# Another periodic order for the steps of a convolution, attention and expert-routing kernel

## The reference

```
x = conv(x)        # channel norm, 1x1 conv, grouped 3x3 conv, softmax state over the image, h, y, 1x1 conv, + x
t = tokens(x)
u = ln(t); q, k, v = lrelu(u Wq + bq), lrelu(u Wk + bk), lrelu(u Wv + bv)
o = softmax(mask(q k^T / 8)) v + u
t = t + gamma * normalised(o) + beta
u = ln(t); expert = argmax(softmax(u gate_w + gate_b))     # 8 experts, capacity 5120 tokens
t = t + prob * (relu(u w1[expert] + b1) w2[expert] + b2)   # kept tokens only
```

## Time and profile before

| | |
|---|---|
| median of 3 runs | 2253.11 us (2244.7 to 2254.15) |
| the profiled execution: its own time, its span | 2252.71 us, 2251.0 us |
| granted TensorE clock, mean | 0.965 |
| busy share of the span: PE, DVE, ACT, POOL | 90%, 84%, 53%, 45% |
| `token_program` | 0 to about 1700 us of the span |
| `finish_program` | about 1700 to 2251 us |
| one period, mean of ten (748.35 to 1226.70 us) | 47.84 us |

### The profile page before, as it was taken

The page is one execution under the profiler, slowest core; times in us unless marked ns, Lnnn a source line. Parts: engine busy times, 40 slices in busy tenths (PEclk is TensorE's granted clock), DMA queues, the critical chain, the costliest instruction groups (busy, mean ns, idle before and its releaser), DMA issues. The chain is left out here.

```text
span 2251.0 us, 42376 instructions
## 1 busy us (share of the span) xinstructions
PE 2021.3 (90%) x13855; PEld 1643.0 (73%) x13855; DVE 1900.7 (84%) x6075; ACT 1196.8 (53%) x2216; POOL 1015.1 (45%) x1276
## 2 busy tenths in 40 slices
PE   1679999999999999999999999999837999999996
PEld 1357777777777777777777777777736999988895
DVE  3268889899998999899999999988865998998895
ACT  0135554555554554554554555554425777777773
POOL 3011443444443444443444434444363665555553
PEclk9679999999999999999999999999967999999998
DMA  4911211121211122111222211221116777877774
GB/s 173 365 48 29 67 48 48 49 71 54 57 57 48 51 74 58 50 56 48 60 65 58 58 48 48 62 67 37 37 35 182 205 222 256 263 248 257 256 246 175
DMA packets 163515, 244.00 MB, mean 108 GB/s; under 512 B 31039, under 2 KB 110478, under 8 KB 163296
## 3 DMA queue, kind: packets, MB, share of 16 engines
q1 hardware_dynamic: 146016, 209.46, 30.7%
q0 software_dynamic: 17280, 31.84, 4.3%
HBM read 115.95 MB, written 95.56 MB: 94 GB/s over the span
## 5 line engine op out<-in xcount | busy, mean ns | idle before, releaser
L1205 PE MATMUL pvp<-va,pT 128*128 128x129 f32 x4096 | 494.6, 276 | 0.6 <-ACT pT L741 0.4
L1205 PEld LDWEIGHTS pvp<-va,pT 128*128 128x128 f32 x4096 | 486.3, 193 | 10.3 <-issue 1.9
L741 ACT ACTIVATE pT<-stp 128x512 f32<-128x512 f32 x512 | 285.3, 595 | 251.4 <-PE stp L1179 245.6
L1376 POOL DMA_INDIRECT token_rows<-res x284 | 305.6, 1076 | 231.0 <-DVE res L1509 161.4
L855 DVE TENSOR_REDUCE mxs<-mxp 128x1 f32<-128x512 f32 x512 | 337.4, 683 | 17.4 <-PE mxp L1082 14.2
L612 POOL TENSOR_TENSOR rstd<-var,neghalf 128x4 f32<-128x4 f32 x128 | 135.5, 1058 | 408.3 <-DVE negm L846 405.7
L1562 PEld LDWEIGHTS e_yp<-w2s,hid 128*128 128x128 f32 x2272 | 294.9, 192 | 20.0 <-ACT hid L1439 0.3
L655 POOL DMA_INDIRECT expert_slots<-rows,slot_i x256 | 267.3, 1044 | 91.6 <-issue 84.8
L1562 PE MATMUL e_yp<-w2s,hid 128*128 128x128 f32 x2272 | 300.5, 276 | 0.0
L1439 ACT ACTIVATE hid<-e_hp,b1c 128x512 f32<-128x512 f32 x284 | 195.2, 687 | 114.7 <-PE e_hp L1554 106.9
L1177 PE MATMUL stp<-qhl,klh 128*128 128x512 f32 x512 | 223.8, 437 | 32.3 <-DMA qhi<-nt 28.9
(11 more groups left out here) (242 smaller groups left out, 3970.7 us busy)
## 6 DMA issues: line engine op xcount, KB each, us to landing
w1p<-w_parts SPq DMA_DIRECT2D x71, 512.0 KB
expert_slots<-fill SPq DMA_DIRECT2D x32, 660.0 KB, 12.0
e_rows<-expert_slots SPq DMA_DIRECT2D x71, 264.0 KB, 2.8
w2s<-in_w SPq DMA_DIRECT2D x71, 256.0 KB
xs<-in_x SPq DMA_DIRECT2D x32, 512.0 KB, 3.6
token_rows<-rows SPq DMA_DIRECT2D x32, 512.0 KB, 3.8
f_rows<-token_rows SPq DMA_DIRECT2D x32, 512.0 KB, 6.9
out<-f_cols SPq DMA_DIRECT2D x32, 512.0 KB, 7.4
```

The source lines that it names most:

```text
L741: a.activation(pT[j][:, kt, :], stp[kt % 2][:], ACT.Exp).then_inc(s["exp_ready"], 1)
L1205: last = mm(pvp[qt % 2][:, 0:VA], pT[c][:, kt, n * P:(n + 1) * P], va[k][:, kt, :], start=(kt == 0), stop=(kt == NT - 1))
L1376: g.indirect_dma_start(out=tokens, out_offset=bass.IndirectOffsetOnAxis(ap=res[n % 2][:, q, TOKEN:TOKEN + 1].bitcast(I32), axis=0), in_=re ...
```

## The change

The lists `head`, `steps` and `tail` are replaced. They hold the same (batch, step) pairs as before, each once; no instruction is added, removed or reshaped. The loop over `steps` runs over passes 4 to 23 and not 5 to 24; it is 20 passes as before. All line numbers behind the lists fall by one. The heart of the diff, with the lists cut:

```
-        steps = [(("ln2n", 2), -1), ("t1b", 0), (("pv", 0, 1), 0), (("ln2n", 3), -1), ("qk_high", 1), ("conv", 2),
-                 ("dt", 2), ("dt_exp", 2), (("mrow", 1), 0), ("mask", 1), ("ln2g", -1), (("pv", 0, 2), 0),
...
+        steps = [(("pv", 1, 2), 0), ("gate", -1), (("pv", 1, 3), 0), (("u1n", 1), 2), (("u1n", 2), 2),
+                 (("mx", 1, 0), 1), (("u1n", 3), 2), (("st", 0, 0), 1), ("gate_turn", -1), (("st", 0, 1), 1),
...
         def passes(eng, one):
             for b, st in head:
                 one(st, *batch(b))
-            for c in range(5, 25):
+            for c in range(4, 24):
                 for st, ahead in steps:
                     one(st, *batch(c + ahead))
             for back, st in tail:
                 one(st, *batch(B - back))
```

More of the change, by code:

```diff
@@ L220, in bc_mid @@
             return ap2.unsqueeze(1).to_broadcast([ap2.shape[0], n, ap2.shape[1]])
-        steps = [(("ln2n", 2), -1), ("t1b", 0), (("pv", 0, 1), 0), (("ln2n", 3), -1), ("qk_high", 1), ("conv", 2),
[13 rows of a table removed]
-                 (("ln2s", 1), 0), (("pv", 0, 0), 1), ("bT_turn", 3), ("qk_lrelu", 2), ("scatter", -1), ("kflag", 2),
-                 (("ln2n", 0), 0), (("ln2n", 1), 0), (("mx", 1, 6), 1), (("mx", 1, 7), 1), (("negmax", 1), 1)]
+        steps = [(("pv", 1, 2), 0), ("gate", -1), (("pv", 1, 3), 0), (("u1n", 1), 2), (("u1n", 2), 2),
[7 rows of a table added]
+                 (("mrow", 1), 1), ("kflag", 2), ("conv", 3), ("qk_high", 2), ("ln2g", 0), ("mask", 2),
[7 rows of a table added]
         def batch(b):
@@ L247, in token_program @@
                 (0, "dt_exp"), (0, "cd_turn"), (0, "h"), (0, "hh"), (0, "g"), (0, "y"), (0, ("ts", 0)),
[2 rows of a table removed]
-                (1, "bcdt"), (1, "bT_turn"), (1, "conv"), (1, "dt"), (1, "dt_exp"), (1, "cd_turn"), (1, "h"),
[8 rows of a table removed]
-                (0, ("st", 0, 7)), (2, "bcdt"), (1, "t1b"), (1, "qk_lrelu"), (0, ("mrow", 1)), (1, "kflag"),
-                (0, ("pv", 0, 0)), (2, "bT_turn"), (0, ("pv", 0, 1)), (1, "qk_high"), (1, "mask"), (1, "qk_low"),
[29 rows of a table removed]
-                (4, "conv"), (3, "mask"), (4, "dt"), (4, "dt_exp"), (2, ("pv", 0, 1)), (2, ("mrow", 1)),
[15 rows of a table removed]
@@ L306, in token_program @@
-                (3, ("pv", 0, 0)), (5, "conv"), (5, "dt"), (5, "dt_exp"), (3, ("mrow", 1)), (4, "mask"), (2, "ln2g"),
[15 rows of a table removed]
-                (6, "conv"), (6, "dt"), (6, "dt_exp"), (4, ("mrow", 1)), (5, "mask"), (3, "ln2g"), (4, ("pv", 0, 2)),
[14 rows of a table removed]
-        tail = [(8, ("ln2n", 2)), (7, "t1b"), (7, ("pv", 0, 1)), (8, ("ln2n", 3)), (6, "qk_high"), (5, "conv"),
[13 rows of a table removed]
-                (6, ("pv", 0, 0)), (5, "qk_lrelu"), (4, "bT_turn"), (8, "scatter"), (5, "kflag"), (7, ("ln2n", 0)),
[32 rows of a table removed]
-                (4, ("negmax", 1)), (3, "kflag"), (5, ("ln2n", 2)), (3, "qk_high"), (3, "qk_low"), (4, ("mrow", 1)),
[15 rows of a table removed]
-                (3, ("pv", 0, 0)), (3, ("negmax", 1)), (1, "conv"), (2, "qk_high"), (4, "ln2g"), (3, ("mrow", 1)),
[13 rows of a table removed]
-                (4, "scatter"), (1, "qk_lrelu"), (2, ("pv", 0, 0)), (1, "mask"), (2, ("mrow", 1)), (3, ("ln2n", 0)),
[13 rows of a table removed]
[12 rows of a table added]
@@ new lines, in token_program @@
+                (0, ("pv", 0, 1)), (2, "bT_turn"), (0, ("mrow", 1)), (0, ("pv", 0, 2)), (1, "qk_high"), (1, "mask"),
[12 rows of a table added]
+                (3, "bcdt"), (2, "qk_lrelu"), (2, "kflag"), (1, ("mx", 1, 7)), (1, ("pv", 0, 0)), (3, "bT_turn"),
[16 rows of a table added]
+                (3, "mask"), (2, ("mrow", 1)), (3, "qk_lrelu"), (3, "qk_high"), (4, "conv"), (1, "ln2g"),
[29 rows of a table added]
+                (6, "bT_turn"), (4, ("negmax", 1)), (3, ("ln2n", 2)), (3, ("ln2n", 3)), (5, "qk_lrelu"),
+                (4, ("pv", 0, 2)), (4, ("mrow", 1)), (5, "kflag"), (6, "conv"), (5, "qk_high"), (3, "ln2g"),
[7 rows of a table added]
@@ new lines, in token_program @@
+        tail = [(8, ("pv", 1, 2)), (9, "gate"), (8, ("pv", 1, 3)), (6, ("u1n", 1)), (6, ("u1n", 2)),
[7 rows of a table added]
+                (6, "kflag"), (5, "conv"), (6, "qk_high"), (8, "ln2g"), (6, "mask"), (7, ("st", 1, 0)), (5, "dt"),
[13 rows of a table added]
+                (6, ("pv", 0, 1)), (6, ("negmax", 1)), (5, "qk_lrelu"), (4, "bT_turn"), (7, ("ln2n", 2)),
+                (7, ("ln2n", 3)), (6, ("pv", 0, 2)), (6, ("mrow", 1)), (4, "conv"), (5, "kflag"), (5, "qk_high"),
+                (7, "ln2g"), (5, "mask"), (6, ("st", 1, 0)), (4, "dt"), (4, "dt_exp"), (5, "qk_low"), (8, "scatter"),
[14 rows of a table added]
+                (4, "qk_lrelu"), (5, ("mrow", 1)), (3, "conv"), (4, "qk_high"), (6, "ln2g"), (5, ("st", 1, 0)),
+                (3, "dt"), (3, "dt_exp"), (4, "mask"), (4, "qk_low"), (7, "scatter"), (5, ("pv", 0, 3)),
[30 rows of a table added]
+                (3, ("st", 1, 1)), (1, "dt"), (1, "dt_exp"), (5, "scatter"), (2, "mask"), (2, "qk_high"),
[13 rows of a table added]
+                (1, "kflag"), (4, "scatter"), (2, ("mrow", 1)), (2, ("pv", 0, 2)), (1, "mask"), (3, ("ln2n", 2)),
[5 rows of a table added]
+                (1, ("mrow", 0)), (3, ("ln3s", 1)), (2, ("pv", 1, 2)), (3, "gate"), (3, "gate_turn"),
[5 rows of a table added]
+                (1, ("negmax", 1)), (1, ("pv", 0, 2)), (3, "scatter"), (1, ("mrow", 1)), (2, ("ln2n", 3)),
@@ L428, in token_program @@
                 (1, ("pv", 0, 3)), (1, ("st", 1, 0)), (1, ("st", 1, 1)), (2, "ln2g"), (2, ("ln3s", 0)),
[3 rows of a table removed]
[3 rows of a table added]
                 (1, ("ln2s", 0)), (1, ("ln2n", 0)), (1, ("ln2s", 1)), (1, ("ln2n", 1)), (1, ("ln2n", 2)), (2, "pos"),
[1 row of a table removed]
-                (1, ("ln3s", 1)), (1, "gate_turn"), (1, "pos"), (1, "scatter")]
[1 row of a table added]
+                (1, "gate"), (1, "gate_turn"), (1, "pos"), (1, "scatter")]
         def passes(eng, one):
```

## The result

The changed kernel takes **2229.47 us** (median of 5 runs, 2228.55 to 2233.13), the one before 2250.07 in the same runs (2244.15 to 2254.15). The ratio is 0.9914, with a 95% interval of 0.9892 to 0.9937: by it the change gains 19 us (the two medians lie 20.6 apart). I had forecast 2222, 31 us faster. So the sign and the range hold, and the size is a third short. The experiments show that the order itself is worth about 55 us, and that a wait which the prediction doesn't name takes some 36 of them back.

The account below looks back on a forecast made before the run. DVE was taken to pace the period, with PE's 45.8 us as floor. Removing the hold of `var` (-33.0 us) and adding 2 for seams gave -31 us, so 2222 us; range 2196 to 2254.

Parts of the forecast that it names:

- DVE paces the period: First program's periods: a microsecond off DVE's own work comes off the 47.84 us period until PE's 45.8 is reached.
- rival (a): More than the hold goes: waits for mrow and ACT shrink, period falls to PE's 45.8, time 2200 us; chance 0.18.
- My floor for it, 45.8: PE's busy time in one period, about 45.8 us, below which the period can't fall with the same PE work.
- The hold of `var`, -33.0 us: DVE's `var` held by POOL's beta addition: 128 instructions, 0.258 us shorter each, all of it gained.
- The place of the addition: POOL's addition kept at 14.4 to 16.8 us behind ln2s, `var` at 18.2: a margin of 1.4 us.
- rival (c): The addition still hits `var`, which is held as before: about 2250 us; chance 0.19 together with rival (b).
- Rival (b): DVE's saved time becomes waits for PE and ACT, 26 us back: 2246 us; chance 0.19 together with rival (c).
- PE's wait for `hs`, mrow's transfer: PE's waits of 0.69 and 1.0 us a period vanish; no extra gain counted, at most 19.5 us for mrow's.
- The mask's transfer: New risk ahead of the first mx: PE waits 0.8 us, covered by DVE; cost 0, at most 1 us a period.
- rival (d): Slower through the mask's transfer landing late: 2274 us if it lands at 4.7 us; chance 0.09.
- Head and tail, +2: Outer batches hold the same steps reordered; 2 us added for seams between lists and remaining single hits.

Follow-up runs that it names:

- e4: The kernel before with the first half of ln3s moved ahead of the cd_turn in the repeated passes: 2233.63 us, ratio 0.9938.
- e1: The changed kernel with SP's store of token rows and load of the next x held until the beta addition is done: 2194.77 us, ratio 0.9773.
- e3: The changed kernel with a third buffer for `t` and SP's store and load held behind the beta addition: 2186.53 us, ratio 0.9733.
- e2: The changed kernel with a third buffer for `t`, transfers left where they are: 2193.26 us, ratio 0.976.
- e7: e3 with the statistics of ln3s moved back ahead of `hs` and `gs` in the repeated passes: 2268.02 us, ratio 1.0101.
- e8: The kernel before with the load of the next x issued right behind the store of token rows in the repeated passes: 2241.88 us, ratio 0.9987.
- e5: The changed kernel with only the load of the next x held behind the beta addition: 2216.24 us, ratio 0.9882.

## Why the prediction came out as it did

*DVE paces the period.* Half right. It held in the old order (e4, where DVE's own waits came up). In the new one, wherever the wait of `t` is gone, the median period falls to PE's pace (45.58 to 45.74 in e1 to e3). That is rival (a), whose mechanism is right but hidden under another. My floor for it, 45.8, was a little high: its ten periods held a stretch of low clock (at 936 us).

*The hold of `var`, -33.0 us.* The mechanism is right: 25 us of it are gone from the instruction, and DVE's busy time is down by 26.9. The price was mis-sized. I took the full length of the hold as time. e4 removes 26 us of it alone and gains 14.5. Elsewhere the length is no measure either way: holds of 2 us cost nothing in the kernel after and nearly their length in e2, and in e7 14 of them cost 4.8 us each, 67 us. The hold is worth what stands behind it on DVE and is needed by PE, and that isn't read from its own row.

*The place of the addition.* This is the step that failed: "POOL's order in between is the same now, so I keep these". POOL's order is the same, but the time is not. The medians over the repeated part: the addition starts 17.7 us behind the second ln2s on DVE, where it was 14.4. Scatter starts 0.5 us later against ln2s, takes 11.1 and not 10.2 us, and lands in 4.1 and not 2.1. POOL's `shift` is held in front of it:

```profile
915.70 1.15 POOL L613 TENSOR_TENSOR shift<-negm,rstd 128x4 f32<-128x4 f32 x1
...
917.01 1.13 POOL L654 DMA_INDIRECT expert_slots<-rows,slot_i  x1 [0.17 <-issue]
```

`shift` usually takes 0.20 us, and 0.48 in this place before; here DVE runs qk_lrelu, which has two inputs in SBUF, beside it. By the Trainium skill's page "SBUF — State Buffer", section "Who interferes with whom", whichever engine issues first keeps the shared ports, so it can hit either side; the trace agrees, 1.15 against 0.20 us on POOL and 1.84 against 0.17 on DVE in the period of e7 shown. I weighed only what holds up DVE and the making of descriptors, took the landing as a constant, and the orders that I set side by side were DVE's and PE's, not SP's, where the load and qk_low's transfers had moved beside the end of scatter. e8 shows that the load with the store is enough for that, 3.95 us in the old order. That the holds went all the same is luck: `var` now stands about 17.4 us behind ln2s (my sum had 18.2), and the late addition starts just behind it at 17.7. With the addition at 15.4 (e1) `var` is held 16 times, as rival (c) had it. Most of these are short, and the six periods with a hold of over 1 us take 46.4 to 46.9 us, where the others take 45.5 to 45.8 (one 46.4).

*What waits for the addition.* I named only `var`. `t` waits for it too, by a buffer shared two batches later. Before, `t` started 3.5 us behind the addition's end (897.01 against 893.50) and never waited for it in ten periods. Now it comes right behind ln3s and one mx. This wait takes 36 of the 55 us. Rival (b), that what DVE no longer loses turns into new waits, has come true, with some 36 us where I had 26, but through this wait and not PE's or ACT's.

*PE's wait for `hs`, mrow's transfer.* Both gone, as said, and counted at 0 for that DVE paced the period. With `t` free they aren't 0: they are the difference between e4's 14.5 and e2's 55, together with DVE's wait for `exT` and the statistics' better place. How much is each one's was not tried.

*The mask's transfer.* PE has no wait for `khi<-kt` above 0.1 us, where I had 0.8 and rival (d) more. Harmless.

*Head and tail, +2.* Wrong in sign. By the starts of the batches' pv the stretch up to batch 5 is 5.2 us shorter, the 20 repeated batches are 8.1 shorter, the tail 7.4; the second program, which the change doesn't touch, is 3.0 shorter, so about that much of the 23.7 between the two profiled spans is spread. The outer parts, which I gave 6 of 26 periods, bring more than the repeated one. Why was not tried.

Open, too: why the store adds 1.4 us to the landing behind qk_low's transfers (e5 against e1), when with no such transfers ahead of it the landing is only 2.1, and why scatter itself takes 0.9 us longer in the new order (e1 has it too, without the store and load behind it).

## What to carry to other kernels

When an order of steps is changed, follow every queue past the places where engines wait for a transfer, the DMA issuer's too: a load that moved by 18 us to beside a store made eight indirect transfers land 2 us later. Ask of each slow operation that moves what waits for its end, buffers above all, and not only what it collides with; a third buffer was worth 36 us in the new order and nothing in the old one. The price of a hold is what stands behind it: holds of the same instruction, all of about 2 us, cost 0, 2.1 or 4.8 us, so find the first instruction behind it that the bounding engine needs. And look at the periods one by one: a median over twenty hides five or six that are 1 to 2 us longer, and a hold can move to the next instruction, from `var` to `negm` or `qkl`, where a count of the first doesn't see it.

## What the runs showed of the hardware

The landing of the same eight indirect transfers, from the end of the last issue to POOL's start, was 1.8 us with qk_low's two transfers alone beside it (e1, e3), 2.1 with the store alone (before), 3.25 with both (e5), 3.95 with store and load (e8), and 4.0 to 4.1 with all of them (e2, after). In all of these qk_low's transfers, where they stand there, go out 2.4 and 1.9 us ahead of the start of the last issue, the store 1.1 to 1.2 and the load 0.2 to 0.5.

A small DVE operation on SBUF that meets POOL's addition is held to its end, whichever it is: `var` up to 2.37 us (before), `negm` 2.36 (e2). `qkl`, which reads two operands in SBUF, took up to 3.38 us instead of 1.22 (e8). In the other direction POOL's `shift` took 1.15 instead of 0.20 us beside DVE's `qk` (after).

In e7 idle time of PE of 2.0 to 3.1 us, in periods where it is otherwise nearly full, was followed by a granted clock of 0.50 for 6.8 us (once 3.4, once 10.2); in the period shown the clock cost more, 3.4 us, than the idle time, 2.65. The kernel before shows such stretches three times in its batches (at 414, 697 and 936 us, the first of 6.8 us), the one after three times for 3.4 us each (its long periods of 49.3 to 50.4 us), e3 not once. The page "TensorE: Matmul & The Clock Gate", section "HAM oscillation — how this bites in real kernels", of the Trainium skill tells of the like for waits on transfers; here it is a copy of 0.21 us behind a held one.
